# Grouped cross attention in a six-stage decoder: the mixing of the values moved ahead of the next tile's key projection, with ACT and DVE reordered alongside

## The chip, the cores and the metric

The kernel runs on one core of one Trainium2 chip. The metric is the device time of one execution in microseconds (us). The kernel before was run three times; a fourth execution was recorded by the hardware profiler. The engines are called as in the profile: PE is TensorE (matmuls), PEld its weight loads, DVE is VectorE, ACT is ScalarE, POOL is GpSimd, SP is SyncE, which issues the DMAs.

## What is computed

The reference is a decoder of two blocks over x of 32 sequences x 64 tokens x 256 features. Each block adds an attention, a cross attention and a feed-forward part to x, each behind a layer norm. The change touches only the fifth of these six parts, the cross attention of the second block:

```python
q = (hidden_states @ Wq + bq).reshape(b, s, NH, HD)           # NH = 16 heads, HD = 128
k = (encoder_hidden_states @ Wk + bk).reshape(b, se, NKV, HD) # NKV = 4, shared by 4 heads each
v = (encoder_hidden_states @ Wv + bv).reshape(b, se, NKV, HD)
q = _rmsnorm(q, qn_w)
k = _rmsnorm(k, kn_w)
scores = jnp.einsum('bhsd,bhed->bhse', q, k) * scale + attention_mask
probs = softmax(scores)
out = jnp.einsum('bhse,bhed->bhsd', probs, v).reshape(b, s, NH * HD) @ Wo
```

## The kernel before, in words

The six parts run one after another, with a barrier between them. The 2048 tokens are 16 tiles of 128 rows, a tile being two sequences of 64 tokens. `grouped_attention` (L1628) runs the fifth part as a software pipeline written out by hand: each engine has a function `turn(t, valid)` that issues its instructions of turn t in a fixed order, for t = -2 to 16; turns 1 to 13 are a hardware loop, the others are unrolled. `valid(k)` says whether tile k exists. An engine carries out its own instructions strictly in this order and waits for the others by semaphores. In turn t the engines score tile t, apply the softmax to it, mix the values and project the output of tile t-1, and project queries, keys and values of tile t+1.

Products are in fp32 split into a high and a low half, three matmuls for each product (`three_passes`, L1624): the high half is a rounded copy made by ACT (or DVE), the low half the difference, made by DVE or POOL.

PSUM has eight banks of 512 columns. Banks 0 and 1 take the projected queries (four groups g = 0 to 3, group g in bank g mod 2) and the transposed queries. Bank 2 takes the keys (`key_or_value(2, ...)`) and the transposed keys, bank 3 the values. Banks 6 and 7 take in turn the scores of tile t, the first half of the mixed values of tile t-1 (`mix(t - 1, 0)`), the scores transposed to rows, and (bank 6) the output projection. Banks 4 and 5 take the second half of the mixed values (`mix(t - 1, 1)`) and the transposed probabilities.

PE in turn t (L2007): the scores of tile t (L2018), 16 matmuls; the key projection of tile t+1 (6 matmuls of 512 columns, L2021 to L2023; in turn -1 the keys of tile 0 are projected at a later place, L2040); the mixing of tile t-1 (`mix`, L1981, matmuls L1988), which waits for `v_lows`, `probsT_lows` and for `scoresT_ready`, ACT's copies of the scores out of banks 6 and 7; the queries of tile t+1, groups 0 to 2, where group 2 waits until DVE has read group 0 out of bank 0 (`q_ready`); the transposes of the scores (L2046); query group 3, which waits for the second of these reads; the output projection of tile t-1 (L2060, L2064); the value projection of tile t+1; the transposes of keys, of the next x and of the scaled queries (L2075, L2080, L2004) and of the probabilities (L2090).

ACT in turn t (L1804): four copies of the scores into `ga_scoresT` (L1812); the squares of the next keys (L1817), which wait for `k_ready` from DVE; `take_mixed` (L1790, L1792) for groups 0 and 1, the rounded copies of the mixed values; logarithm and exponential for the keys' norm, `ga_k_inv` (L1826, L1828); `take_mixed` for groups 2 and 3; the rounded copy of the values (L1836); squares of the queries, the softmax's exponential, the queries' norm, then the copies behind the transposes.

DVE in turn t (L1906): the normalised x of tile t+2; `key_steps(t + 1)` (L1887), that is `ga_k_raw`, the bias addition for the keys, which waits for the key projection, and `ga_k_sum`, which waits for ACT's squares; `mixed_low` (L1893, L1897) for groups 0 and 1, which wait for both rounded copies of their half; `biased` (L1876, L1878) for query group 0; the low half of the values (L1920); `biased` for groups 1 and 2; mask and maximum; `biased` for group 3; `mixed_low` for groups 2 and 3; sums, reciprocal and so on.

POOL subtracts the maxima, scales the queries (L1746), makes the low half of the context (L1739), and in turns -1 and 0 the low halves of w_v and w_o. SP loads one context tile per turn, when POOL has finished the low half of the one before.

Of the kernel before, what the change touches and what calls it, by code (L numbers as in the profile page):

```python
# [26 lines left out]
ACT = mybir.ActivationFunctionType  # L27
# [1600 lines left out]
def grouped_attention(core, raw, w_q_high, w_q_low):  # L1628
# [9 lines left out]
    nc, dram, ps, ident = core.nc, core.dram, core.psum, core.ident  # L1638
    with ExitStack() as scope:
# [4 lines left out]
        w_k_high, w_k_low = sb("w_k_high", [P, KC, KV_COLS], F32R), sb("w_k_low", [P, KC, KV_COLS], F32R)  # L1644
# [11 lines left out]
        k_raw, k_squares, kT = (sb(name, [P, KV_COLS]) for name in ("k_raw", "k_squares", "kT"))  # L1656
# [48 lines left out]
        def started(t, first):  # L1705

            return not isinstance(t, int) or t >= first
# [67 lines left out]
        @block.scalar  # L1775
        def _(act):
            ln.on_scalar(act)

            def square(n, g):
                act.wait_ge(q_ready, 4 * n + (g + 1))  # L1780
                nc.scalar.activation(q_scaled[:, g * G_CHUNK:(g + 1) * G_CHUNK], q[:, g * G_CHUNK:(g + 1) * G_CHUNK], ACT.Square).then_inc(squares_ready, 1)  # L1781

            def query_rms(n, half):
                heads = slice(HALF * half, HALF * (half + 1))
                act.wait_ge(q_sums, 2 * n + (half + 1))
                nc.scalar.activation(q_log[:, heads], q_sum[:, heads], ACT.Ln, bias=rms_eps[:], scale=1.0 / G_HD).then_inc(q_logs, 1)
                act.wait_ge(q_logs, 2 * n + (half + 1))
                nc.scalar.activation(q_inv[:, heads], q_log[:, heads], ACT.Exp, scale=-0.5).then_inc(q_invs, 1)  # L1788

            def take_mixed(n, j):  # L1790
                act.wait_ge(mixed_psum, 2 * n + (j // 2 + 1))
                nc.scalar.activation(mixed_rows(mixedT_high, j), mixed_of(j).rearrange("p b (h t) -> p b h t", h=G_GROUP), ACT.Identity, bias=bias_v[:, j:j + 1]).then_inc(mixed_highs, 1)  # L1792

            def context_high(n):
                act.wait_ge(ctx_ready, 16 * n + 16)
                if started(n, 1):
                    act.wait_ge(v_psum, n)
                nc.scalar.copy(ctxT_high[:], ctxT[:]).then_inc(ctx_highs, 1)

            def take_queries(n, g):  # L1800
                act.wait_ge(qT_psum, 4 * n + (g + 1))
                nc.scalar.copy(qT[:, 4 * g:4 * g + 4].rearrange("p h t -> p (h t)"), ps[:, g % 2, :]).then_inc(qT_ready, 1)

            def turn(t, valid):  # L1804
                if isinstance(t, int) and t == -1:
                    act.wait_ge(loaded, LOADS)
                    act.wait_ge(consts_set, 2)
                if valid(t):
                    act.wait_ge(scored, t + 1)
                    act.wait_ge(k_invs, t + 1)  # L1810
                    for j in range(G_KV):
                        done = nc.scalar.activation(scoresT[:, j * E:(j + 1) * E], ps[:, 6 + j // 2, (j % 2) * E:(j % 2 + 1) * E], ACT.Copy,  # L1812
                                                    scale=k_inv[:, j:j + 1])
                    done.then_inc(scoresT_ready, 1)
                if valid(t + 1):
                    act.wait_ge(k_ready, t + 2)
                    nc.scalar.activation(k_squares[:], k_raw[:], ACT.Square).then_inc(k_squared, 1)  # L1817
                if isinstance(t, int) and t == -1:
                    act.wait_ge(w_v_loaded, 16)
                    nc.scalar.copy(w_v_high[:], w_v).then_inc(w_v_highs, 1)  # L1820
                if valid(t - 1):
                    take_mixed(t - 1, 0)
                    take_mixed(t - 1, 1)
                if valid(t + 1):
                    act.wait_ge(k_sums, t + 2)
                    nc.scalar.activation(k_log[:], k_sum[:], ACT.Ln, bias=rms_eps[:], scale=1.0 / G_HD).then_inc(k_logs, 1)  # L1826
                    act.wait_ge(k_logs, t + 2)
                    nc.scalar.activation(k_inv[:], k_log[:], ACT.Exp, scale=-0.5).then_inc(k_invs, 1)  # L1828
                if valid(t - 1):
                    take_mixed(t - 1, 2)  # L1830
                    take_mixed(t - 1, 3)
                if valid(t):
                    if started(t, 1):
                        act.wait_ge(mixed_psum, 2 * t)
                    act.wait_ge(v_psum, t + 1)
                    nc.scalar.copy(values_high[:], ps[:, 3, :]).then_inc(v_highs, 1)  # L1836
                if valid(t + 1):
                    for g in range(4):
                        square(t + 1, g)
                if valid(t):  # L1840
                    act.wait_ge(shifted, t + 1)
                    nc.scalar.activation(probs[:], probs[:], ACT.Exp).then_inc(exp_done, 1)
                if valid(t + 1):
                    query_rms(t + 1, 0)
                    query_rms(t + 1, 1)
                    act.wait_ge(kT_psum, t + 2)
                    nc.scalar.activation(kT[:], ps[:, 2, :], ACT.Copy, scale=gain[:]).then_inc(kT_ready, 1)
                if valid(t + 2):
                    act.wait_ge(xT_psum, t + 3)
                    nc.scalar.copy(xT_high[:], ps[:, 7, 0:E]).then_inc(xT_highs, 1)  # L1850
                if isinstance(t, int) and t == -2:
                    act.wait_ge(w_k_loaded, 16)
                    nc.scalar.copy(w_k_high[:], w_k).then_inc(w_k_highs, 1)
                if valid(t + 2):
                    context_high(t + 2)
                if valid(t + 1):
                    take_queries(t + 1, 0)
                    take_queries(t + 1, 1)
                if valid(t):
                    act.wait_ge(probsT_psum, t + 1)  # L1860
                    nc.scalar.copy(probsT_high[:].rearrange("p (b c) -> p b c", b=2), ps[:, 4:6, :]).then_inc(probsT_highs, 1)
                if valid(t + 1):
                    take_queries(t + 1, 2)
                    take_queries(t + 1, 3)

            pipeline(act, turn)

        @block.vector
        def _(dve):
# [17 lines left out]
            def key_steps(n):  # L1887
                dve.wait_ge(k_psum, n + 1)
                nc.vector.tensor_tensor(k_raw[:], ps[:, 2, :], bias_k[:], ALU.add).then_inc(k_ready, 1)
                dve.wait_ge(k_squared, n + 1)  # L1890
                nc.vector.tensor_reduce(k_sum[:], k_squares[:].rearrange("p (j d) -> p j d", d=G_HD), AX.X, ALU.add).then_inc(k_sums, 1)

            def mixed_low(n, j):  # L1893
                dve.wait_ge(mixed_highs, 4 * n + (j // 2 * 2 + 2))
                for b in range(2):
                    high, low = (mixed_rows(half, j)[:, b] for half in (mixedT_high, mixedT_low))
                    done = nc.vector.scalar_tensor_tensor(low, mixed_of(j)[:, b], bias_v[:, j:j + 1], high.bitcast(F32), ALU.add, ALU.subtract)  # L1897
                done.then_inc(mixed_lows, 1)
# [7 lines left out]
            def turn(t, valid):  # L1906
                if isinstance(t, int) and t == -1:
                    gains()
                if valid(t + 2):
                    ln.normalise(xn[:], t + 2).then_inc(xn_ready, 1)  # L1910
                if valid(t + 1) and started(t, 0):
                    key_steps(t + 1)
                if valid(t - 1):
                    mixed_low(t - 1, 0)
                    mixed_low(t - 1, 1)
                if valid(t + 1):
                    biased(t + 1, 0)
                if valid(t):
# [51 lines left out]
        def _(pe):  # L1970
# [36 lines left out]
            def turn(t, valid):  # L2007
                if valid(t):
# [9 lines left out]
                            done = nc.tensor.matmul(ps[half, 6 + j // 2, (j % 2) * E:(j % 2 + 1) * E], kT[:, j * P + SEQ * b:j * P + SEQ * b + SEQ],  # L2018
                                                    qT[:, 4 * j:4 * j + 4, SEQ * b:SEQ * b + SEQ], start=True, stop=True)
                    done.then_inc(scored, 1)  # L2020
                if valid(t + 1) and started(t, 0):  # L2021
                    pe.wait_ge(ctx_lows, t + 2)
                    key_or_value(2, w_k_high, w_k_low, k_psum)  # L2023
                if valid(t - 1):
                    pe.wait_ge(v_lows, t)
                    pe.wait_ge(probsT_lows, t)
                    if valid(t):
                        pe.wait_ge(scoresT_ready, t + 1)
                    else:
                        pe.wait_ge(x_ready, t)  # L2030
                    mix(t - 1, 0)
                    mix(t - 1, 1)
                if valid(t + 1):
                    pe.wait_ge(xT_ready, t + 2)
                    for g in range(3):
                        query(t + 1, g)
# [624 lines left out]
```

## Time and profile before

| | |
|---|---|
| median of three runs | 1464.93 us (1462.18 to 1465.11) |
| profiled execution | 1476.43 us, of it 1474.7 us span |
| busy in the span | PE 1293.8 us (88%), PEld 1040.3 (71%), DVE 984.3 (67%), ACT 716.6 (49%), POOL 426.6 (29%) |
| the stage of the change | from about 761 to 1170 us of the span |
| turns 1 to 14 | 23.3 us each, from 810.58 to 1136.61 us |

A row of the time order gives start, length, engine, line and operation with the tiles written and read; behind it in brackets stands how long the engine had been idle and what ended that. Several alike instructions in a row are merged (x4), with their length from the first start to the last end. Matmuls overlap each other, so a matmul's length is longer than the distance to the next start. A copy's printed end also overlaps the start of the next on its engine by about 0.1 us.

### The profile page before, as it was taken

To read this page: it belongs to the slowest core of one execution; us is meant where nothing else is said; L and a number is where in the kernel's file an instruction comes from. 1 tells how busy PE (TensorE), PEld (TensorE's weight loads), DVE (VectorE), ACT (ScalarE), POOL (GpSimd) and SP (SyncE) were. 2 spreads that over 40 slices of the span, in tenths; PEclk is the share of its full clock that TensorE was granted. 3 is DMA by queue.
4 is the path that set the end of the run, shared out by engine and by line. 5 is a ranking of instruction groups with operands and counts; after the bars stand their busy time and mean duration, and the time that the engine had idled before them with its cause. 6 is when DMAs were issued, how large, how long until landed. Compare 5 with 4: busy or idle time off the path is not lost. (4 is left out here: it accounts for less than half of the span.)

```text
span 1474.7 us, 28031 instructions
## 1 busy us (share of the span) xinstructions
PE 1293.8 (88%) x9996; PEld 1040.3 (71%) x9996; DVE 984.3 (67%) x1866; ACT 716.6 (49%) x1487; POOL 426.6 (29%) x498
## 2 busy tenths in 40 slices
PE   4888987199999995689977999999999599999998
PEld 3666665045555554378956788787887599999998
DVE  4777676267777654669855777787776557655555
ACT  1555555047777773432015565656556245333332
POOL 1112120344444310056645332332323021112210
PEclk9999999569999998579988999999999799999999
DMA  3000000345445310010030000000000110010001
GB/s 107 1 0 0 0 0 1 79 106 140 108 121 131 98 35 7 26 70 1 0 112 24 6 7 4 7 4 7 7 4 1 44 43 23 22 36 30 2 1 58
DMA packets 49003, 54.31 MB, mean 37 GB/s; under 512 B 7365, under 2 KB 44837, under 8 KB 46245
## 3 DMA queue, kind: packets, MB, share of 16 engines
q1 hardware_dynamic: 48936, 53.41, 13.0%
q8 instruction: 43, 0.70, 0.2%
q14 instruction: 24, 0.20, 0.0%
HBM read 42.52 MB, written 10.49 MB: 36 GB/s over the span
## 5 line engine op out<-in xcount | busy, mean ns | idle before, releaser
L677 DVE TENSOR_REDUCE fa_neg_max<-psum 128x2 f32<-128x512 f32 x256 | 168.0, 689 | 66.4 <-PE psum L853 65.6
L737 ACT ACTIVATE fa_probs<-psum 128x1024 f32<-128x1024 f32 x128 | 130.4, 1019 | 43.9 <-PE psum L864 40.6
L1624 PE MATMUL psum<-mo_xT_high,mo_w_high 128*128 128x256 f32 x512 | 145.6, 284 | 3.8 <-DVE mo_w_low L2297 3.8
L1624 PE MATMUL psum<-mo_xT_low,mo_w_high 128*128 128x256 f32 x512 | 145.2, 284 | 0.0
L1624 PE MATMUL psum<-mo_xT_high,mo_w_low 128*128 128x256 f32 x512 | 144.6, 282 | 0.0
L853 PE MATMUL psum<-fa_k_stack,fa_q_stack 72*128 72x256 bf16 x512 | 106.6, 294 | 36.5 <-DMA fa_k_stack<-k_parts 35.3
L2252 ACT ACTIVATE mo_silu<-psum 128x256 f32<-128x256 f32 x128 | 49.2, 384 | 159.3 <-PE psum L1624 159.3
L2386 DVE TENSOR_TENSOR mo_mid<-mo_silu,psum 128x256 f32<-128x256 f32 x128 | 53.7, 419 | 96.6 <-ACT mo_silu L2252 96.4
L1624 PEld LDWEIGHTS psum<-mo_xT_high,mo_w_high 128*128 128x128 f32 x512 | 97.4, 190 | 4.2 <-DVE mo_w_low L2297 4.2
L853 PEld LDWEIGHTS psum<-fa_k_stack,fa_q_stack 72*128 72x128 bf16 x512 | 42.0, 102 | 79.5 <-DVE fa_neg_max L677 33.6
L1624 PEld LDWEIGHTS psum<-mo_xT_low,mo_w_high 128*128 128x128 f32 x512 | 97.5, 190 | 0.0
L1624 PEld LDWEIGHTS psum<-mo_xT_high,mo_w_low 128*128 128x128 f32 x512 | 97.4, 190 | 0.0
L1757 POOL TENSOR_TENSOR ga_probs<-ga_probs,ga_top 128x1024 f32<-128x1024 f32 x16 | 30.5, 1906 | 209.6 <-DVE ga_top L1931 209.6
L864 PE MATMUL psum<-fa_q_stack,fa_k_stack 75*128 75x256 bf16 x512 | 81.4, 283 | 7.6 <-DMA fa_q_stack<-fa_max_rows 7.6
L258 POOL TENSOR_TENSOR da_keys<-da_rot,da_head_mask 128x1024 f32<-128x1024 f32 x16 | 30.4, 1899 | 186.9 <-DVE da_rot L386 186.9
L2199 POOL TENSOR_TENSOR mo_w_low<-mo_raw,mo_w_high 128x512 fp32r<-128x512 f32 x21 | 27.6, 1314 | 188.0 <-ACT mo_w_high L2227 188.0
L1746 POOL TENSOR_TENSOR ga_q_scaled<-ga_q,ga_q_inv 128x1024 f32<-128x1024 f32 x32 | 70.1, 2192 | 35.4 <-ACT ga_q_inv L1788 35.4
L878 PE MATMUL psum<-fa_probs,fa_values 128*32 128x256 f32 x1024 | 72.2, 401 | 1.1 <-ACT fa_probs L737 1.1
L1624 PE MATMUL psum<-mo_w_high,mo_mid_high 128*128 128x256 f32 x256 | 72.3, 282 | 0.0
L1624 PE MATMUL psum<-mo_w_low,mo_mid_high 128*128 128x256 f32 x256 | 71.9, 281 | 0.0
L1624 PE MATMUL psum<-mo_w_high,mo_mid_low 128*128 128x256 f32 x256 | 71.7, 280 | 0.0
L1781 ACT ACTIVATE ga_q_scaled<-ga_q 128x512 f32<-128x512 f32 x64 | 40.1, 632 | 60.5 <-DVE ga_q L1878 60.4
(400 smaller groups left out, 3655.5 us busy)
## 6 DMA issues: line engine op xcount, KB each, us to landing
fa_q_stack<-q_parts SPq DMA_DIRECT2D x16, 576.0 KB
fa_k_stack<-k_parts SPq DMA_DIRECT2D x16, 576.0 KB
k_parts<-fa_parts SPq DMA_DIRECT2D x80, 64.0 KB, 2.7
q_parts<-fa_parts SPq DMA_DIRECT2D x48, 64.0 KB, 5.3
x<-in_x SPq DMA_DIRECT2D x4, 512.0 KB, 5.6
fa_context<-in_ctx SPq DMA_DIRECT2D x16, 128.0 KB, 2.2
staged<-in_ga_w_q SPq DMA_DIRECT2D x1, 2048.0 KB, 10.3
ga_ctxT<-in_ctxT SPq DMA_DIRECT2D x16, 128.0 KB, 2.2
```

The source lines that it names most:

```text
L258: nc.gpsimd.tensor_tensor(keys[:], rot[:, None, 2 * P:3 * P].to_broadcast([P, D_HEADS // 2, P]), head_mask[:, :, None].to_broadcast([P, D_ ...
L677: nc.vector.tensor_reduce(neg_max[:, b, :, h], ps[:, h % 2, :].rearrange("p (q k) -> p q k", q=2), AX.X, ALU.max, negate=True).then_inc(ma ...
L737: nc.scalar.activation(probs[:, g].rearrange("p h k q -> p h (k q)"), ps[:, 2 + 2 * (g % 2):4 + 2 * (g % 2), :], ACT.Exp).then_inc(exp_don ...
L853: done = nc.tensor.matmul(ps[:, h % 2, q * E:(q + 1) * E], q_stack[0:MAX_ROW, slot, b, h, q * P:(q + 1) * P], k_stack[0:MAX_ROW, slot, b, ...
L864: done = nc.tensor.matmul(ps[:, 2 + 2 * (g % 2) + h, k * E:(k + 1) * E], k_stack[0:STACK_ROWS, slot, b, 2 * g + h, k * P:(k + 1) * P], q_s ...
L878: done = nc.tensor.matmul(ps[32 * c:32 * c + 32, 6, half * E:(half + 1) * E], values[:, slot, k, 8 * b + h, :], probs[:, h // 2, h % 2, k, ...
L1624: done = nc.tensor.matmul(out, lhsT[i], rhs[j], start=start and k == 0, stop=stop and k == 2)
L1746: nc.gpsimd.tensor_tensor(q_scaled[:, columns].rearrange("p (h d) -> p h d", d=G_HD), q[:, columns].rearrange("p (h d) -> p h d", d=G_HD), ...
L1757: nc.gpsimd.tensor_tensor(probs[:], probs[:], top[:, :, None].to_broadcast([P, G_HEADS, SEQ]), ALU.subtract).then_inc(shifted, 1)
L1781: nc.scalar.activation(q_scaled[:, g * G_CHUNK:(g + 1) * G_CHUNK], q[:, g * G_CHUNK:(g + 1) * G_CHUNK], ACT.Square).then_inc(squares_ready, 1)
L2252: nc.scalar.activation(silu[:, j % 4], ps[:, j % 4, 0:2 * P], ACT.Silu).then_inc(silu_ready, 1)
L2386: nc.vector.tensor_tensor(mid[:, j % 4], silu[:, j % 4], ps[:, j % 4, 2 * P:4 * P], ALU.mult).then_inc(mid_ready, 1)
```

## The change

In the turns, PE's key projection of tile t+1 moves from ahead of to behind the mixing of tile t-1. DVE's `key_steps(t + 1)` moves behind `mixed_low` of groups 0 and 1. On ACT the squares of the keys move behind `take_mixed` 0 and 1 (and, in turn -1, behind the rounded copy of w_v), and `take_mixed` 2 and 3 move from behind `ga_k_inv` to ahead of the keys' logarithm. No instruction, wait or tile is added or removed.

```diff
@@ -1812,23 +1812,23 @@
                         done = nc.scalar.activation(scoresT[:, j * E:(j + 1) * E], ps[:, 6 + j // 2, (j % 2) * E:(j % 2 + 1) * E], ACT.Copy,
                                                     scale=k_inv[:, j:j + 1])
                     done.then_inc(scoresT_ready, 1)
-                if valid(t + 1):
-                    act.wait_ge(k_ready, t + 2)
-                    nc.scalar.activation(k_squares[:], k_raw[:], ACT.Square).then_inc(k_squared, 1)
                 if isinstance(t, int) and t == -1:
                     act.wait_ge(w_v_loaded, 16)
                     nc.scalar.copy(w_v_high[:], w_v).then_inc(w_v_highs, 1)
                 if valid(t - 1):
                     take_mixed(t - 1, 0)
                     take_mixed(t - 1, 1)
+                if valid(t + 1):
+                    act.wait_ge(k_ready, t + 2)
+                    nc.scalar.activation(k_squares[:], k_raw[:], ACT.Square).then_inc(k_squared, 1)
+                if valid(t - 1):
+                    take_mixed(t - 1, 2)
+                    take_mixed(t - 1, 3)
                 if valid(t + 1):
                     act.wait_ge(k_sums, t + 2)
                     nc.scalar.activation(k_log[:], k_sum[:], ACT.Ln, bias=rms_eps[:], scale=1.0 / G_HD).then_inc(k_logs, 1)
                     act.wait_ge(k_logs, t + 2)
                     nc.scalar.activation(k_inv[:], k_log[:], ACT.Exp, scale=-0.5).then_inc(k_invs, 1)
-                if valid(t - 1):
-                    take_mixed(t - 1, 2)
-                    take_mixed(t - 1, 3)
                 if valid(t):
                     if started(t, 1):
                         act.wait_ge(mixed_psum, 2 * t)
@@ -1908,11 +1908,11 @@
                     gains()
                 if valid(t + 2):
                     ln.normalise(xn[:], t + 2).then_inc(xn_ready, 1)
+                if valid(t - 1):
+                    mixed_low(t - 1, 0)
+                    mixed_low(t - 1, 1)
                 if valid(t + 1) and started(t, 0):
                     key_steps(t + 1)
-                if valid(t - 1):
-                    mixed_low(t - 1, 0)
-                    mixed_low(t - 1, 1)
                 if valid(t + 1):
                     biased(t + 1, 0)
                 if valid(t):
@@ -2018,9 +2018,6 @@
                             done = nc.tensor.matmul(ps[half, 6 + j // 2, (j % 2) * E:(j % 2 + 1) * E], kT[:, j * P + SEQ * b:j * P + SEQ * b + SEQ],
                                                     qT[:, 4 * j:4 * j + 4, SEQ * b:SEQ * b + SEQ], start=True, stop=True)
                     done.then_inc(scored, 1)
-                if valid(t + 1) and started(t, 0):
-                    pe.wait_ge(ctx_lows, t + 2)
-                    key_or_value(2, w_k_high, w_k_low, k_psum)
                 if valid(t - 1):
                     pe.wait_ge(v_lows, t)
                     pe.wait_ge(probsT_lows, t)
@@ -2030,6 +2027,9 @@
                         pe.wait_ge(x_ready, t)
                     mix(t - 1, 0)
                     mix(t - 1, 1)
+                if valid(t + 1) and started(t, 0):
+                    pe.wait_ge(ctx_lows, t + 2)
+                    key_or_value(2, w_k_high, w_k_low, k_psum)
                 if valid(t + 1):
                     pe.wait_ge(xT_ready, t + 2)
                     for g in range(3):
```

## Rows read from the trace of the kernel before

**Rows 1.** Busy time of turn 5: stretch, length, engines (instructions), clock, DMA share, GB/s.

```profile
903.72:927.00 23.28, 22.86 (x163) 18.86 (x162) 17.52 (x27) 14.16 (x31) 7.02 (x4) 1.00 0.02 6
```

**Rows 2.** PE in time order, turn 5: start us, length us, engine, line, operation.

```profile
903.72 1.95 PE L2018 MATMUL psum<-ga_qT,ga_kT 128*64 128x256 f32 x16
905.60 0.49 PE L1624 MATMUL psum<-ga_w_k_high,ga_ctxT_high 128*128 128x512 f32 x1
...
907.42 0.39 PE L1988 MATMUL psum<-ga_probsT_high,ga_values_high 64*128 64x256 f32 x2 [0.16 <-ACT ga_scoresT L1812]
...
909.00 0.50 PE L1624 MATMUL psum<-w_q_high,ga_xT_high 128*128 128x512 f32 x1
...
911.42 0.39 PE L1624 MATMUL psum<-w_q_high,ga_xT_low 128*128 128x512 f32 x1
911.65 0.40 PE L1624 MATMUL psum<-w_q_low,ga_xT_high 128*128 128x512 f32 x1
912.15 0.50 PE L1624 MATMUL psum<-w_q_high,ga_xT_high 128*128 128x512 f32 x1
...
914.44 0.48 PE L1624 MATMUL psum<-w_q_high,ga_xT_high 128*128 128x512 f32 x1
```

**Rows 3.** PE in time order, turn 0.

```profile
790.63 0.50 PE L1624 MATMUL psum<-ga_w_k_high,ga_ctxT_high 128*128 128x512 f32 x1
...
792.14 0.40 PE L1624 MATMUL psum<-w_q_high,ga_xT_high 128*128 128x512 f32 x1
```

**Rows 4.** ACT in time order, turn 5.

```profile
905.71 1.57 ACT L1812 ACTIVATE ga_scoresT<-psum,ga_k_inv 128x256 f32<-128x256 f32 x4 [0.91 <-PE psum L2018]
908.02 0.63 ACT L1817 ACTIVATE ga_k_squares<-ga_k_raw 128x512 f32<-128x512 f32 x1 [0.74 <-DVE ga_k_raw L1889]
...
910.14 1.25 ACT L1792 ACTIVATE ga_mixedT_high<-psum,ga_bias_v 128x512 fp32r<-128x512 f32 x2
911.28 0.59 ACT L1836 CAST ga_values_high<-psum 128x512 fp32r<-128x512 f32 x1
```

**Rows 5.** DVE in time order, turn 5.

```profile
907.30 0.69 DVE L1889 TENSOR_TENSOR ga_k_raw<-psum,ga_bias_k 128x512 f32<-128x512 f32 x1 [1.57 <-PE psum L1624]
908.69 0.69 DVE L1891 TENSOR_REDUCE ga_k_sum<-ga_k_squares 128x4 f32<-128x512 f32 x1 [0.70 <-ACT ga_k_squares L1817]
909.84 1.66 DVE L1897 SCALAR_TENSOR_TENSOR ga_mixedT_low<-psum,ga_bias_v,ga_mixedT_high 128x256 fp32r<-128x256 f32 x4 [0.47 <-ACT ga_mixedT_high L1792]
911.42 0.68 DVE L1878 TENSOR_TENSOR ga_q<-psum,ga_bias_q 128x512 f32<-128x512 f32 x1
912.02 0.68 DVE L1920 TENSOR_TENSOR ga_values_low<-psum,ga_values_high 128x512 fp32r<-128x512 f32 x1
```

**Rows 6.** All engines in time order, turn 15 (no keys left to project).

```profile
1140.32 0.38 PE L1988 MATMUL psum<-ga_probsT_high,ga_values_high 64*128 64x256 f32 x2 [1.76 <-ACT ga_scoresT L1812]
...
1141.32 2.42 ACT L1792 ACTIVATE ga_mixedT_high<-psum,ga_bias_v 128x512 fp32r<-128x512 f32 x4 [1.15 <-PE psum L1988]
...
1142.62 1.66 DVE L1897 SCALAR_TENSOR_TENSOR ga_mixedT_low<-psum,ga_bias_v,ga_mixedT_high 128x256 fp32r<-128x256 f32 x4 [4.89 <-ACT ga_mixedT_high L1792]
...
1144.43 0.96 PE L2046 MATMUL psum<-ident,ga_scoresT 128*128 128x128 f32 x4 [2.46 <-DVE ga_mixedT_low L1897]
```

**Rows 7.** All engines in time order, end of turn -1.

```profile
782.40 0.47 PE L1624 MATMUL psum<-ga_w_v_high,ga_ctxT_high 128*128 128x512 f32 x1 [3.74 <-POOL ga_w_v_low L1761]
...
783.05 3.75 POOL L1746 TENSOR_TENSOR ga_q_scaled<-ga_q,ga_q_inv 128x1024 f32<-128x1024 f32 x2 [0.79 <-ACT ga_q_inv L1788]
...
787.68 1.15 PE L2004 MATMUL psum<-ident,ga_q_scaled 128*128 128x128 f32 x8 [0.52 <-ACT ga_qT L1802]
```

**Rows 8.** Busy time and clock: an earlier stage, and the end of this one.

```profile
470.00:480.00 10.00, 8.60 (x81) 5.14 (x79) 7.03 (x13) 6.53 (x12) 3.00 (x9) 0.95 0.69 182
480.00:490.00 10.00, 9.98 (x96) 5.95 (x96) 6.32 (x12) 7.50 (x13) 4.82 (x10) 0.88 0.23 59
1145.00:1150.00 5.00, 3.68 (x17) 3.28 (x16) 3.68 (x6) 0.00 (x0) 1.16 (x1) 0.50 0.02 3
```

More of the change, by code:

```diff
@@ L1910, in turn @@
                     ln.normalise(xn[:], t + 2).then_inc(xn_ready, 1)
-                if valid(t + 1) and started(t, 0):
-                    key_steps(t + 1)
                 if valid(t - 1):
@@ L1915, in turn @@
                     mixed_low(t - 1, 1)
+                if valid(t + 1) and started(t, 0):
+                    key_steps(t + 1)
                 if valid(t + 1):
@@ L2020, in turn @@
                     done.then_inc(scored, 1)
-                if valid(t + 1) and started(t, 0):
-                    pe.wait_ge(ctx_lows, t + 2)
-                    key_or_value(2, w_k_high, w_k_low, k_psum)
                 if valid(t - 1):
@@ L2032, in turn @@
                     mix(t - 1, 1)
+                if valid(t + 1) and started(t, 0):
+                    pe.wait_ge(ctx_lows, t + 2)
+                    key_or_value(2, w_k_high, w_k_low, k_psum)
                 if valid(t + 1):
```

## The prediction

> **What bounds the kernel now.** The change touches one stage, the cross attention, so I read that stage, not the page's averages. It is a pipeline of turns; turn t scores tile t, mixes the values of tile t-1 and projects the queries, keys and values of tile t+1. First view: the busy time of one turn, 903.72 to 927.00 (turn 5) [rows 1]. It lasts 23.28 us and PE works in 22.86 of them at a granted clock of 1.00; DVE and ACT have 6 to 9 us to spare. So PE's own order sets the pace: whatever makes PE wait is paid in full, save where it removes one of the 0.42 us in which PE waits today.
>
> Second view: PE in order of time [rows 2]. After the scores come the six key matmuls from 905.60, the mixing at 907.42, queries 0 and 1 from 909.00, query 2 at 912.15, query 3 at 914.44. Two waits matter. The mixing waits 0.16 us for ACT's copies of the scores (ga_scoresT), because its first half goes into banks 6 and 7, which hold the scores. And between the last matmul of query 1 (911.65, a stride of 0.23, so done streaming at 911.88) and 912.15 PE waits 0.27 us: query 2 reuses bank 0 and needs DVE's first bias addition. The key matmuls are thus what PE does while ACT empties the scores' banks: 905.71 to 907.28 [rows 4].
>
> **The change on PE.** Nothing is added or removed; in turns that have both a mixing and a key projection the two swap. Those are t = 1 to 14, 14 turns. The mixing cannot start sooner: its last wait is for ga_scoresT, and no row lets that copy begin earlier. Turn 15, which has no keys to project, shows the new order: there PE waits 1.76 us ahead of the mixing [rows 6]. So the mixing stays at 907.42, its 1.58 us end at 909.00, and the keys, which were hidden, stand open behind it. They cost 1.51 us: in turn 0 they start at 790.63 and the query behind them at 792.14 [rows 3]. Queries 0 and 1 then end at 911.88 + 1.51 - 0.10 = 913.29 (the 0.10 is the longer first matmul after a change of group, 0.50 against 0.40 us, which the keys now pay).
>
> **The change on DVE and ACT.** Query 2 needs DVE's first bias addition, and that now has the keys' chain just ahead of it. Step by step: ACT takes the first mixed half 1.00 us after the mixing starts and DVE follows at 2.30 us (1140.32, 1141.32, 1142.62) [rows 6], so at 908.42 and 909.72. DVE's four low parts hold it for 1.58 us (909.84 to 911.42) [rows 5]: to 911.30. The keys are in PSUM 1.70 us after their start (905.60 to 907.30) [rows 2, 5], at 910.70, so DVE comes last and ga_k_raw starts at 911.30. ACT squares it 0.72 us later (907.30 to 908.02) [rows 4, 5]: 912.02. Its sum on DVE starts 0.67 us later: 912.69. The next DVE operation of this length starts 0.60 us behind (911.42 to 912.02): bias addition 0 at 913.29. Query 2 starts 0.73 us after that (911.42 to 912.15) [rows 2, 5]: 914.02. Against 912.15 that is **1.87 us per turn**: 1.14 for the open keys net of the recovered 0.27, and 0.73 of new waiting behind the keys' chain.
>
> What is queued behind? On ACT the square now stands ahead of the third and fourth mixed copies and waits for the keys, so ACT is idle from about 909.7 to 912.02. Before, ga_values_high started 3.26 us after the square (908.02 to 911.28); two mixed copies fewer are behind it (1.14 us, 910.14 to 911.28) [rows 4], so it starts at 912.02 + 2.12 = 914.14 and ends at 914.73. DVE's low values (0.68) and bias addition 1 follow; query 3 could start at 914.73 + 0.68 + 0.73 = 916.14. PE reaches it at 914.02 + 2.29 = 916.31 (912.15 to 914.44) [rows 2], so that move costs nothing, with only 0.17 us of cover; without it, the excess would be paid. Everything later (mask, maximum, exponential, output projection, POOL's scaling) hangs on query 2, query 3 or the transposes between them and shifts as one. ga_k_inv is wanted only by the next turn's scores. No DMA moves: SP's context loads wait for POOL's ctxT_low, which stays at the turn's end.
>
> **The start-up.** In turn -1 the copy of w_v no longer stands behind the keys' square, so POOL's w_v_low is early and the 3.74 us that PE waits for it at 782.40 vanish [rows 7]. But the next PE step, the transposes of the scaled queries, waits for POOL, whose two scalings run 783.05 to 786.80 whatever PE does. They release the second pair of transposes at 786.86 instead of 787.68: a gain of 0.8 us at best. Against it: PE now idles before 785 rather than before 782.4, with the clock, halved after such a wait, covering other work, and DVE's long cast of w_o may meet POOL's scaling. Nearest rows give that up to the 1.7 us of one clock fall (below) plus 0.8 lost. I take 0, ends -0.8 and +2.5.
>
> **The sum.** 14 x 1.87 = 26.2 us, start-up 0. The profiled execution took 1476.43 us (span 1474.7), so the changed one should take about 1502.6. The median of the runs shown, 1464.93, is 11.5 lower; nothing in the sum depends on what makes that difference, so 1464.9 + 26.2 = **1491.1**. Bounds: 1.14 us per turn if DVE is in time, and about 2.1 if each of five handovers is 0.05 longer, that is 16.0 to 29.4 us; with the start-up's ends 15 to 32.
>
> **A rule on the clock.** The row first: turn 15's wait of 1.76 us left the clock alone, and only after the wait of 2.46 us at 1144.43 did it read 0.50 (1145 to 1150) [rows 6, 8]. The changed turn has a wait of 1.76 us with the same neighbours, so the sum takes no clock loss. The Trainium skill ("TensorE: Matmul & The Clock Gate", section "A second HAM failure mode: psum-queue depth-cycling") says that a PE which idles briefly and often between groups of matmuls on cycled PSUM banks swings between its two clock levels. That is this change's pattern; by one wait the trace disagrees, by fourteen it has not been asked.
>
> **Rivals.**
> (a) *Only PE's part is paid.* DVE's bias addition is in time because the keys' chain is shorter than I add up: 14 x 1.14 = 16.0, so 1480.9. For it: four short handovers make up the 0.73. Against: each is read from a row of this loop, and the order is fixed by the diff. Chance 0.08.
> (b) *The clock falls.* Mechanism: each of the 14 waits of 1.76 us is followed by a second of 0.73, and some bring PE from 2.4 to 1.2 GHz. Price: the two rows with one fall read 0.95 and 0.88 over 10 us each [rows 8], so 0.5 + 1.2 = 1.7 us. In half of the turns 12 us more: 1503. The rule above would be this one. Against: the single like wait. Chance 0.08.
> (c) *Faster.* Place: the fronts of the turns and turn -1. If the mixing did not have to wait for ACT (its wait under 0.42 us), earlier mixed values would remove PE's other waits: 14 x 0.42 = 5.9 and 0.8 at the start, 1458.2. It decides from the point where ACT's copies finish within 0.4 us of the scores; the row of turn 15 says 1.76. Chance 0.02.
> (d) *Nothing.* The swap is absorbed, as it would be if DVE or ACT were the bound, or if the mixing's wait ran on regardless: 1465. Against: 22.86 of 23.28. Chance 0.02.
> My forecast has 0.80.
>
> **How the numbers follow.** About 0.2% (3 us) is what a measurement of this kernel can tell from no change. The forecast itself spans 1485 to 1497. Reaching down to (a) and up to a few clock falls gives 1479 to 1500; outside lie most of (b), all of (c) and (d). Slower by over 0.2%: forecast, (a), (b), 0.96; same 0.02; faster 0.02.
>
> **What would show it.** In the changed profile: turns of 25.15 us instead of 23.28; PE idle about 1.76 us ahead of L1988 "<-ACT ga_scoresT" in every turn; ga_k_raw idle on PE gone (1.57 us today) [rows 5] and the wait of query 2 for ga_q at 0.7 instead of 0.27; ACT idle some 2.3 us before the square. The clock should stay 1.00. A turn of 24.4 would be (a), clock below 1 in the middle of the stage (b), and a mixing that starts under 3.6 us after the scores would sink the argument.

## The result, and the profile after

The changed kernel was measured at 1495.84 us (median of four, 1494.6 to 1513.9) against 1465.02 us; ratio 1.0244, 95% interval 1.0165 to 1.0323. The interval is wide, and its centre high, because of one execution of 1513.9 us at a mean clock of 0.928, of which there is no trace: the ratio is one of means, 1500.0 to 1464.3 us, and without that execution the mean would be 1495.4. Measured again in the experiments, six executions gave 1495.27 us against 1468.56; ratio 1.0164, interval 1.0136 to 1.0193, that is 20 to 28 us slower. The profiled execution took 1496.84 us (span 1495.1).

The changed kernel's turn 5, in the form of [rows 1]:

```profile
904.28:929.43 25.15, 22.75 (x163) 18.98 (x163) 17.33 (x27) 14.09 (x31) 7.02 (x4) 1.00 0.02 5
```

The turn lasts 25.15 us instead of 23.28, and the clock stays 1.00. PE's time order of this turn, to be laid beside [rows 2]:

```profile
904.28 1.95 PE L2018 MATMUL psum<-ga_qT,ga_kT 128*64 128x256 f32 x16
907.99 0.39 PE L1988 MATMUL psum<-ga_probsT_high,ga_values_high 64*128 64x256 f32 x2 [1.76 <-ACT ga_scoresT L1812]
...
909.57 0.50 PE L1624 MATMUL psum<-ga_w_k_high,ga_ctxT_high 128*128 128x512 f32 x1
...
911.08 0.39 PE L1624 MATMUL psum<-w_q_high,ga_xT_high 128*128 128x512 f32 x1
...
913.64 0.39 PE L1624 MATMUL psum<-w_q_low,ga_xT_high 128*128 128x512 f32 x1
914.59 0.50 PE L1624 MATMUL psum<-w_q_high,ga_xT_high 128*128 128x512 f32 x1 [0.56 <-DVE ga_q L1878]
...
916.87 0.48 PE L1624 MATMUL psum<-w_q_high,ga_xT_high 128*128 128x512 f32 x1
```

What the forecast put at 907.42, 909.00, 910.51 and 914.02 on the old turn's scale is here 3.71, 5.29, 6.80 and 10.31 us behind the start of the scores; the forecast's distances from 903.72 are 3.70, 5.28, 6.79 and 10.30. ACT and DVE, to be laid beside [rows 4] and [rows 5]:

```profile
906.28 1.57 ACT L1812 ACTIVATE ga_scoresT<-psum,ga_k_inv 128x256 f32<-128x256 f32 x4 [0.97 <-PE psum L2018]
908.99 1.27 ACT L1792 ACTIVATE ga_mixedT_high<-psum,ga_bias_v 128x512 fp32r<-128x512 f32 x2 [1.15 <-PE psum L1988]
912.58 0.63 ACT L1823 ACTIVATE ga_k_squares<-ga_k_raw 128x512 f32<-128x512 f32 x1 [2.32 <-DVE ga_k_raw L1889]
913.12 1.25 ACT L1792 ACTIVATE ga_mixedT_high<-psum,ga_bias_v 128x512 fp32r<-128x512 f32 x2
...
914.73 0.59 ACT L1836 CAST ga_values_high<-psum 128x512 fp32r<-128x512 f32 x1
```

```profile
910.29 1.66 DVE L1897 SCALAR_TENSOR_TENSOR ga_mixedT_low<-psum,ga_bias_v,ga_mixedT_high 128x256 fp32r<-128x256 f32 x4 [4.05 <-ACT ga_mixedT_high L1792]
911.87 0.68 DVE L1889 TENSOR_TENSOR ga_k_raw<-psum,ga_bias_k 128x512 f32<-128x512 f32 x1
913.25 0.69 DVE L1891 TENSOR_REDUCE ga_k_sum<-ga_k_squares 128x4 f32<-128x512 f32 x1 [0.70 <-ACT ga_k_squares L1823]
913.85 0.68 DVE L1878 TENSOR_TENSOR ga_q<-psum,ga_bias_q 128x512 f32<-128x512 f32 x1
915.35 0.69 DVE L1920 TENSOR_TENSOR ga_values_low<-psum,ga_values_high 128x512 fp32r<-128x512 f32 x1 [0.82 <-ACT ga_values_high L1836]
```

ACT waits 2.32 us for the keys with two mixed copies queued behind their squares. DVE adds the keys' bias directly behind the low parts, sums the squares, and only then comes to bias addition 0 at 913.85. PE waits for its end behind query 1: 0.56 us by the row, which counts from the modelled end of the last matmul; counted as in the forecast (913.64 + 0.23 to 914.59) it is 0.72.

The lengths of whole parts differ as well. First the kernel before, then the changed one; the three stretches are the second sublayer, which the change does not touch, the whole stage of the change, and the end of that stage from the scores of turn 15:

```profile
262.80:566.60 303.80, 251.74 (x2336) 150.45 (x2336) 196.79 (x361) 194.12 (x322) 118.90 (x260) 0.88 0.39 99
760.00:1171.50 411.50, 378.04 (x2592) 311.43 (x2592) 285.00 (x444) 228.63 (x468) 128.84 (x76) 0.96 0.05 16
1136.61:1171.50 34.89, 22.83 (x177) 20.69 (x176) 16.25 (x31) 9.81 (x17) 1.90 (x1) 0.85 0.00 1
```

```profile
262.70:556.90 294.20, 245.35 (x2336) 147.69 (x2336) 196.09 (x361) 194.06 (x322) 118.95 (x260) 0.90 0.40 103
751.30:1191.70 440.40, 377.17 (x2592) 314.32 (x2592) 283.92 (x442) 229.29 (x468) 128.62 (x76) 0.95 0.05 15
1155.85:1191.70 35.85, 23.88 (x177) 21.91 (x176) 16.21 (x29) 9.81 (x17) 1.90 (x1) 0.81 0.00 1
```

The stage grew by 28.9 us, the span by 20.4 only, mainly because the profiled execution before had spent 9.6 us more in the second sublayer.

### The profile page after: what moved, and what is told of

Same layout as the page of the kernel before. It is cut to its first block and busy times, and to the rows that moved or that the text cites. A ratio compares the mean times of both kernels' runs of the same rounds, so it can differ in the third digit from the quotient of the medians.

```text
span 1495.1 us, 28031 instructions
## 1 busy us (share of the span) xinstructions
PE 1286.1 (86%) x9996; PEld 1039.7 (70%) x9996; DVE 982.3 (66%) x1866; ACT 717.0 (48%) x1487; POOL 426.3 (29%) x498
## 5 line engine op out<-in xcount | busy, mean ns | idle before, releaser
L1897 DVE SCALAR_TENSOR_TENSOR ga_mixedT_low<-psum,ga_bias_v,ga_mixedT_high 128x256 fp32r<-128x256 f32 x128 | 52.9, 476 | 64.5 <-ACT ga_mixedT_high L1792 64.5
```

## The experiments

Turn lengths are distances between the starts of the first score matmuls (L2018 in the kernel before) of turns 1 to 15; from the same execution they repeat within 0.1 us, unless the clock falls or a first turn differs.

**The changed kernel again** (no edit).

> The changed kernel as it is, to see how its time spreads. Theory A (the wait chain of the turn alone): turns of 25.15 us in every execution, granted clock 1.00 through turns 1 to 14; executions then differ only as those of the kernel before do, and nearly all lie at 1494 to 1497. Rival B (the clock falls in some executions at the 1.76 us waits): some executions of 1505 to 1515 at a mean clock of 0.93 or less, and if the profile falls on one, single turns of more than 26 us with the clock under 1. Rival C: such slow executions come from the second sublayer, whose length differed by 9.6 us between the two profiles, and the kernel before has them as often.

Measured: turns of 25.14 to 25.19 us, all 14; executions from 1489.05 to 1497.71 us, clock 0.936 to 0.945. Theory A holds. No execution like the one of 1513.9 came again, so its cause stays open: nothing of it was recorded but time and clock. The kernel before, run beside the later experiments, has one execution of 1482.02 us at a clock of 0.931, 15.6 us above the median of its 17, so such an execution need not come from the change.

**PE's move alone.** The kernel before with the key projection behind `mix(t - 1, 1)`; DVE and ACT unchanged.

> Only PE's keys move behind the mixing; DVE and ACT keep the order of before. Theory A (handovers added up from the rows of before): the keys are in PSUM at 910.70 on turn 5's scale, ga_k_raw at once, the squares at 911.42, only then ACT's first two mixed copies (911.96), DVE's low parts at 913.24, bias addition 0 at 914.82, query 2 at 915.55 instead of 912.15: 3.40 us per turn, turns of 26.68, 14 of them 47.6 us. Rival (only PE's open keys are paid): turns of 24.4 us, 16 us in all, whatever the others' order.

Measured: nine turns of 26.68 to 26.73 us, five of 28.2 to 28.3; 1523.37 us, ratio 1.0378 (1.0341 to 1.0415). PE's waits over most of the stage:

```profile
PE psum L1624 <- DVE ga_q L1878: 27.3, 13, 2.1
PE psum L1988 <- ACT ga_scoresT L1812: 21.1, 12, 1.8
```

The short turns are as added up: 3.4 us each, or 48 us. The five long ones are clock falls. One of them, in PE's time order of turn 4, shows a stride (the distance from one matmul's start to the next) of 0.43 us behind the wait, where it is 0.23 in the short turns:

```profile
890.26 0.61 PE L1624 MATMUL psum<-w_q_high,ga_xT_high 128*128 128x512 f32 x1 [2.10 <-DVE ga_q L1878]
890.67 0.63 PE L1624 MATMUL psum<-w_q_high,ga_xT_low 128*128 128x512 f32 x1
891.10 0.63 PE L1624 MATMUL psum<-w_q_low,ga_xT_high 128*128 128x512 f32 x1
```

So the reordering of DVE and ACT "to match" does its part: it takes 1.55 us out of each turn of this kernel. It repairs less than PE's move costs.

**DVE's and ACT's orders alone.** The changed kernel with PE's keys put back ahead of the mixing.

> Only DVE and ACT change their order; PE keeps the keys ahead of the mixing. Theory A: query 2 waits for bias addition 0, and that stands behind DVE's low parts (from 909.72) and the keys' chain whether or not PE has moved, so it starts at 914.02 as in the changed kernel: turns of 25.15 us, 26 us in all. Rival (PE's open keys are what is paid, as 1.14 of the 1.87 us): turns near 24.0 us (0.73 more than before) or unchanged at 23.28.

Measured: six turns of 25.13 to 25.20 us, eight of 26.3 to 26.8; 1506.04 us, ratio 1.0253 (1.0213 to 1.0293). The short turns are those of the changed kernel though PE has not moved at all. DVE's chain from the mixing to bias addition 0 sets query 2, and PE's later keys fit underneath it. PE's time order in turn 2, and the clock in three stretches around it (columns as in [rows 1]):

```profile
840.15 0.40 PE L1624 MATMUL psum<-w_q_low,ga_xT_high 128*128 128x512 f32 x1
842.49 0.50 PE L1624 MATMUL psum<-w_q_high,ga_xT_high 128*128 128x512 f32 x1 [1.94 <-DVE ga_q L1878]
...
843.29 0.40 PE L1624 MATMUL psum<-w_q_high,ga_xT_high 128*128 128x512 f32 x1
843.52 0.59 PE L1624 MATMUL psum<-w_q_high,ga_xT_low 128*128 128x512 f32 x1
843.91 0.63 PE L1624 MATMUL psum<-w_q_low,ga_xT_high 128*128 128x512 f32 x1
```

```profile
840.00:843.50 3.50, 1.56 (x7) 0.97 (x6) 1.99 (x4) 2.98 (x7) 0.00 (x0) 1.00 0.00 0
843.50:847.00 3.50, 3.50 (x14) 2.99 (x13) 2.44 (x4) 1.50 (x3) 0.00 (x0) 0.51 0.00 0
847.00:850.00 3.00, 3.00 (x24) 2.83 (x23) 2.97 (x5) 0.60 (x1) 1.16 (x1) 1.00 0.00 0
```

PE waits 1.94 us, after no wait longer than 0.2 us in this turn; 1.0 us after the wait a stride of 0.23 becomes 0.4, and the clock reads 0.51 for 3.5 us.

**The copy of w_v alone.** The kernel before with these lines exchanged on ACT:

```diff
+                if isinstance(t, int) and t == -1:
+                    act.wait_ge(w_v_loaded, 16)
+                    nc.scalar.copy(w_v_high[:], w_v).then_inc(w_v_highs, 1)
                 if valid(t + 1):
                     act.wait_ge(k_ready, t + 2)
                     nc.scalar.activation(k_squares[:], k_raw[:], ACT.Square).then_inc(k_squared, 1)
-                if isinstance(t, int) and t == -1:
-                    act.wait_ge(w_v_loaded, 16)
-                    nc.scalar.copy(w_v_high[:], w_v).then_inc(w_v_highs, 1)
```

> Kernel before with only ACT's copy of w_v in turn -1 ahead of the keys' squares. Theory A (start-up term measured as +1.8 us in the changed kernel's profile, a clock fall on the transposes and scores of turn 0): the scores of tile 0 start 29.7 us after the stage begins instead of 28.7, turn 0 lasts 22.6 instead of 21.8, turns 1 to 14 stay at 23.28; total 1 to 2 us longer than before. Rival (the freed 3.74 us wait is worth something): 0.8 us shorter.

Measured: scores of tile 0 29.3 us after the stage's first DVE instruction, turn 0 22.9 us, turns 1 to 14 23.3 us; 1466.14 against 1468.56 us, ratio 0.9977 (0.9957 to 0.9997). The trace shows the lengthening of 1.7 us in the start-up, the executions a small gain; the profiled execution, 1475.68 us, was the slowest of the twelve. Which of them holds on average is not settled. The two start-up figures together are 50.6, 50.8 and 50.2 us in the profiles of three kernels with the old place of the copy, and 50.6 to 53.1 (mean 52.1) in eight with the new one.

**The keys split on DVE.** The changed kernel, with `key_steps` split into its two halves, `key_raw` (the bias addition) and `key_sum` (the sum of the squares). The diff shows DVE's turns; the two definitions, and the place in turn -1, where both halves stay together, are left out:

```diff
                 if valid(t + 1) and started(t, 0):
-                    key_steps(t + 1)
+                    key_raw(t + 1)
                 if valid(t + 1):
                     biased(t + 1, 0)
+                if valid(t + 1) and started(t, 0):
+                    key_sum(t + 1)
```

> The changed kernel, but on DVE the keys' bias addition, then bias addition 0 of the queries, then the keys' sum. Theory A: query 2 no longer waits behind the keys' chain and starts at 913.29 on turn 5's scale, as the open keys alone allow (1.14 us late instead of 1.87); but ACT's copy of the values still stands behind the keys' squares and two mixed copies, so bias addition 1 is in time for query 3 only at 916.11: turns of 24.95 us, 0.2 less than in the changed kernel. Rival (the 0.73 us behind the keys' chain are all there is): turns of 24.42.

Measured: turns of 25.11 to 25.14 us; 1504.82 us in one execution, in whose trace the stage begins 9.7 us later than in the changed kernel's (760.98 against 751.30 us). DVE, and PE's query 3:

```profile
896.39 0.68 DVE L1889 TENSOR_TENSOR ga_k_raw<-psum,ga_bias_k 128x512 f32<-128x512 f32 x1
897.19 0.69 DVE L1878 TENSOR_TENSOR ga_q<-psum,ga_bias_q 128x512 f32<-128x512 f32 x1
897.80 0.68 DVE L1893 TENSOR_REDUCE ga_k_sum<-ga_k_squares 128x4 f32<-128x512 f32 x1
899.86 0.69 DVE L1924 TENSOR_TENSOR ga_values_low<-psum,ga_values_high 128x512 fp32r<-128x512 f32 x1 [1.38 <-ACT ga_values_high L1836]
900.47 1.28 DVE L1878 TENSOR_TENSOR ga_q<-psum,ga_bias_q 128x512 f32<-128x512 f32 x2
```

```profile
901.20 0.50 PE L1624 MATMUL psum<-w_q_high,ga_xT_high 128*128 128x512 f32 x1 [0.39 <-DVE ga_q L1878]
```

Bias addition 0 (897.19) is 0.8 us behind the keys' instead of 2.0, and still nothing is won. As expected the wait moves on: the values' low half waits for ACT (899.86), bias addition 1 follows, query 3 waits 0.39 us for it. The 0.2 us expected besides are lost because bias addition 2 and the mask stand behind the same chain.

**The values' copy moved up as well.** The kernel with the split keys, and on ACT `values_high` directly behind `take_mixed(t - 1, 1)`.

> As split_keys, and ACT copies the values directly behind the first two mixed copies, in the time in which it waited for the keys. Theory A: nothing is left but PE's own exposure of the keys, 1.51 us less 0.10 and the 0.27 of the old wait for bias addition 0: turns of 24.42 us, 1.14 more than before, 16 us in all. Rival (the copies of the scores or the mixing set the turn): no change against split_keys.

Measured: turns of 24.32 to 24.39 us (one 24.65); 1487.76 us, ratio 1.0124 (1.0069 to 1.0179), that is 10 to 26 us, in which the 15 us of the turns lie. One of its turns:

```profile
908.37:932.70 24.33, 22.43 (x163) 18.98 (x162) 17.43 (x27) 14.00 (x31) 7.01 (x4) 1.00 0.02 5
```

The 0.1 us less than forecast is the long first matmul of query 2, which is gone when PE does not wait there. With the DVE and ACT chain out of the way the open keys alone remain, net of PE's old wait for bias addition 0: 1.05 us per turn.

**Half of the mixing first.** The changed kernel with, on PE (and ACT's waits for `mixed_psum` to match):

```diff
                     pe.wait_ge(probsT_lows, t)
+                    mix(t - 1, 1)
                     if valid(t):
                         pe.wait_ge(scoresT_ready, t + 1)
                     else:
                         pe.wait_ge(x_ready, t)
                     mix(t - 1, 0)
-                    mix(t - 1, 1)
```

> The changed kernel, with the second half of the mixing (banks 4 and 5, which need no copy of the scores) ahead of the wait for ga_scoresT. It halves PE's wait ahead of the mixing from 1.76 to about 0.9 us and ends the mixing and the keys 0.8 us sooner. Theory A: the turn does not get shorter, since the first half still starts at 907.42, and DVE and ACT run the same chain from there to bias addition 0: turns of 25.15 us, the wait of query 2 longer by what the mixing won, about 1.5. Rival (PE's waiting for the scores' copies is what is paid): turns of 24.3. On the clock: no single wait over 1.8 us, so it stays 1.00.

Measured: turns of 25.05 to 25.07 us, but for the first (25.28) and the last (25.14); 1494.46 us in one execution. PE's two waits in one turn:

```profile
882.65 0.39 PE L1988 MATMUL psum<-ga_probsT_high,ga_values_high 64*128 64x256 f32 x2 [0.76 <-ACT ga_scoresT L1812]
...
889.26 0.50 PE L1624 MATMUL psum<-w_q_high,ga_xT_high 128*128 128x512 f32 x1 [1.24 <-DVE ga_q L1878]
```

The wait ahead of the first half fell from 1.76 to 0.76 us, and the wait of query 2 grew from 0.56 to 1.24. The 0.08 us that the turn did gain go with the first half, which starts 3.61 us behind the scores instead of 3.71. The longest new wait of the changed kernel, the one that its profile shows first, is not what its turn costs.

**Both repairs together.**

> The changed order of PE with both repairs: the second half of the mixing ahead of the wait for ga_scoresT, and the orders of DVE and ACT of relaxed. Theory A: relaxed alone was bound by PE (24.33), half_first alone by DVE's and ACT's chain (25.07); together PE ends the mixing, keys and queries 0 and 1 0.8 us sooner, about 912.5 on turn 5's scale, and bias addition 0, now behind the keys' bias addition only, allows query 2 at about 912.6 instead of 912.15: turns of 23.7 us, still 0.4 over the kernel before. Rival (either repair alone already gives all there is): 24.3 or 25.1.

Measured: turns of 23.68 to 23.75 us; 1475.15 against 1470.03 us, ratio 1.0040 (1.0018 to 1.0062). The two repairs add up only together (0.08 and 0.82 us singly, 1.46 as a pair), and the order "mixing, then keys" is still 0.4 us per turn slower than the order before.

**A version faster than both.** The kernel before with, on DVE:

```diff
                     mixed_low(t - 1, 0)
-                    mixed_low(t - 1, 1)
                 if valid(t + 1):
                     biased(t + 1, 0)
+                if valid(t - 1):
+                    mixed_low(t - 1, 1)
```

> Kernel before, with bias addition 0 on DVE between the low parts of mixed groups 0 and 1. Theory A: the query's group 0 is in PSUM by 910.69, DVE adds its bias at 910.67 instead of 911.42, and PE goes from query 1 to query 2 without the wait of 0.27 us: turns of 23.01 us, 3.8 us in all, 0.26% faster than the kernel before. Rival (the 0.27 us come back as a longer wait of the output projection for the mask, or of query 3): 23.28 as before.

Measured: turns of 22.90 to 22.98 us; 1462.47 against 1466.41 us (12 and 17 executions), ratio 0.9952 (0.9924 to 0.9980). DVE:

```profile
895.10 0.88 DVE L1897 SCALAR_TENSOR_TENSOR ga_mixedT_low<-psum,ga_bias_v,ga_mixedT_high 128x256 fp32r<-128x256 f32 x2 [0.47 <-ACT ga_mixedT_high L1792]
895.94 0.69 DVE L1878 TENSOR_TENSOR ga_q<-psum,ga_bias_q 128x512 f32<-128x512 f32 x1
896.55 0.86 DVE L1897 SCALAR_TENSOR_TENSOR ga_mixedT_low<-psum,ga_bias_v,ga_mixedT_high 128x256 fp32r<-128x256 f32 x2
```

The wait of 0.27 us and the long first matmul are both gone: 0.36 us per turn, 5 us in all.

## Why the prediction was right or wrong

**Right, step by step: the turn.** 1.87 us per turn were added up from the rows of before, and the changed turn is 1.87 us longer. The open keys, the chain from the low parts to bias addition 0 and the shift of the rest all stand in the trace at the forecast distances; the run with the values' copy moved up prices the first (1.05 net, 1.14 forecast), and the run with DVE's and ACT's orders alone shows that the second suffices for the whole 1.87. Of the rivals, (a) and (d) fell with the turn, (c) with the wait of 1.76 us, which is still there in each turn. Rival (b) fell for the changed kernel (no turn shows a fall), but the clock does fall in its two sister kernels, PE's move alone and the others' orders alone.

**Wrong: the ends.** "I take 0" for the start-up is the term of the sum that failed. In both traces of the changed kernel it is 1.8 us; in the first the scores of tile 0 came 1.0 us later and turn 0 lasted 0.8 longer. The forecast had its cause in the upper bound and left it out of the sum. The changed kernel's end of turn -1:

```profile
775.27 3.75 POOL L1746 TENSOR_TENSOR ga_q_scaled<-ga_q,ga_q_inv 128x1024 f32<-128x1024 f32 x2 [8.09 <-ACT ga_q_inv L1788]
...
777.31 3.80 PE L2004 MATMUL psum<-ident,ga_q_scaled 128*128 128x128 f32 x16 [4.21 <-POOL ga_q_scaled L1746]
777.53 3.64 DVE L1957 CAST ga_w_o_high<-staged 128x4096 fp32r<-128x4096 f32 x1
...
781.04 2.74 PE L2018 MATMUL psum<-ga_qT,ga_kT 128*64 128x256 f32 x16
```

PE, early with the values, waits 4.21 us for POOL, and the clock reads 0.50 from 776 to 782 us. Then sixteen transposes take 3.80 us, and sixteen score matmuls 2.74 us instead of 1.95. The half clock makes 1.6 of the 1.8 us: the second eight transposes took about 1.9 us instead of 1.08, and from the first score matmul to the key projection it was 2.67 us instead of 1.87, both at full clock before. The hoped-for gain of 0.8 us did not come either, because POOL's scalings began 24.0 us behind the stage's first DVE instruction instead of 23.0; of that, 0.5 us is DVE's wait for the load of the mask, which ended later. That the loss holds on average is not shown: the twelve executions with the copy of w_v alone do not have it. The end of the stage, which I did not cost, is 0.96 us longer with the same instructions; its clock reads 0.81 instead of 0.85, and it lasted 33.1 to 38.5 us over the kernels run. What places the clock falls there stays open. Together 26.2 + 1.8 + 1.0 = 29.0, against 28.9 of the stage. The whole executions are less sharp than the traces: the forecast was 26.2 us on top of the kernel before, the medians of the first comparison differ by 30.8 and those of the second by 26.7 (its means by 24.8).

**Wrong: the top of the range.** The first comparison's ratio puts the changed kernel at 1465.02 x 1.0244 = 1500.8 us, just outside the range of 1479 to 1500. It is the execution of 1513.9 us that takes it there: with the other three alone the ratio is 1.0212, or 1496.1 us. The range reached up to "a few clock falls" in the turns and the start-up and had no term for such an execution, whose cause is unknown. The forecast also took 3 us for what a measurement of this kernel can tell from no change, while 17 executions of the kernel before, in one experiment, lie between 1464.68 and 1476.23 us. And its "1485 to 1497" does not follow from its own bounds: 15 to 32 us on 1464.9 are 1480 to 1497.

**POOL and DVE in the start-up.** The feared meeting took place, but DVE gave way: its cast of w_o took 3.64 us (2.29 before), and POOL, which had started first, finished its scalings in 3.75 us as before [rows 7]. (So the Trainium skill has it, "SBUF — State Buffer", section "SBUF: two separate sides": whichever of the two starts first holds the shared port pair for its whole instruction.) So the meeting did not lengthen POOL's scalings, on which PE waits; the loss is in the main the clock's.

**The rule on the clock.** With a wait of 1.76 us in each turn the granted clock stayed at 1.00 from turn 2 to turn 14; with 1.94 us, in the kernel with DVE's and ACT's orders alone, it fell in 8 turns of 14. The Trainium skill tells of a kernel whose PE, idling briefly and often between groups of matmuls on cycled PSUM banks, swings between its two levels ("TensorE: Matmul & The Clock Gate", section "A second HAM failure mode: psum-queue depth-cycling"). The changed kernel does not do so; its sister does.

## What to carry to other kernels

Before work is moved out of a gap, ask what the gap waits for: the keys were free because they covered ACT's 1.57 us of copies, and behind the mixing they stand open (1.51 us, of which 1.05 are left once PE's old waits are netted out). Then follow each in-order engine past the moved step to the first result that the bottleneck needs (here bias addition 0, then bias addition 1, then the mask); the price is set by the later of the two paths, so repairing one path alone, even the one with the largest wait in the profile, may win nothing. A wait of 0.3 us in front of a bottleneck can be removed by letting the one small operation it needs go ahead of a long one on the other engine.

## What the hardware showed

PE's clock can fall after a shorter wait than the 2.46 us of the one fall whose wait the rows of before show [rows 6, 8]. In four profiles with a wait of 1.76 us in each of 14 turns, no turn from 2 on was longer than the others by more than 0.1 us, and the waits left the clock at 1.00. With a single long wait of 1.94 us per turn, 8 of 14 turns fell to half clock; with one of 1.76 and one of 2.10, 5 of 14. The same wait left the clock alone in the remaining turns, so its length is not all that decides; what else does was not tested. Each fall costs 1.2 to 1.6 us. So in their profiles the two reorderings that keep PE waiting for 1.9 us and more were slower by another 8 to 11 us than by their waits alone. Between 1.76 and 1.94 us nothing was tried.
